# A compositional interaction network on one core: all four full steps of its first layer in high and low halves, and a summation tree whose first level is done by accumulating transfers

## The chip, the core and the metric

The kernel runs on one core of a Trainium2 chip. The metric is device time in microseconds (us) of one execution: 946.62 us, the median of three runs (946.28 to 947.04). The profile is of one further execution, which took 947.22 us, of which the recorded span is 945.3 us.

## The reference

For 512 samples, 32 embeddings of 32 numbers are gathered from 32 tables. Two layers of a compositional interaction network follow, and a three-layer perceptron:

```python
e = jnp.stack([tbl_0[ids[:, 0]], ..., tbl_31[ids[:, 31]]], axis=1)      # (512, 32, 32)
x0 = prev = e
for W in (filter_0, filter_1):                # (1, 32*32, 128), (1, 32*128, 128)
    z = jnp.einsum('bhd,bmd->bhmd', x0, prev).reshape(b, h * m, d)
    cur = jax.nn.relu(jnp.einsum('bpd,pn->bnd', z, W[0]))
    prev = cur; outs.append(cur)
z = jnp.sum(jnp.concatenate(outs, axis=1), axis=-1)                      # (512, 256)
h = jnp.concatenate([z, dense_ctx], axis=1)
h = jnp.maximum(h @ W_top1 + b_top1, 0.0)
h = jnp.maximum(h @ W_top2 + b_top2, 0.0)
y = h @ W_top3
```

All of it is float32. A product of two float32 matrices can be had on TensorE in one float32 instruction pair, or as three passes in the type fp32r, where each factor is split into a high part (the value rounded to fp32r) and a low part (the rest): high x high, low x high, high x low.

## The kernel before

The batch is cut into 4 blocks of 128 samples, the embedding dimension into 8 groups of 4; that makes 32 chunks of 4 x 128 = 512 columns. While chunk c is in layer 2, chunk c+1 is in layer 1 and chunk c+2 is being fetched and spread. Every engine runs an order that is written out by hand in slots.

**Layer 2.** A chunk has two halves q = 0 and 1 (a "pair" of tiles ab = 0, 1, each 128 samples wide), a half has four rounds e = 0 to 3, and a round has four slots for TensorE: slot 16q + 4e + 2ab + kind. In each TensorE multiplies cur (128 x 128) with 512 columns of the second filter in three passes (line 836) into a bank. Kind 0 banks go to ScalarE, which scales four 128-column pieces by a field of x0 and puts them side by side in parts (line 521); its slots are 16q + 4e + ab. Kind 1 banks go to VectorE, which adds its eight scaled pieces of a round into acc (line 721); its slots are 16q + 4e. The last of VectorE's additions of a half lands in parts too. ScalarE has one bank per tile, VectorE two, so TensorE may be about two rounds ahead of VectorE. Each half leaves two tiles of parts, 128 x 2048, whose 16 pieces of 128 must be summed: GpSimd halves each three times (line 352: 1024, 512 and 256 wide), which leaves two pieces, called left. parts has two buffers, so ScalarE may write the same buffer again two halves later, once the first level has read it (the wait on tree). In the next chunk ScalarE copies one piece of left into a bank (line 455, slot 20), VectorE adds the other (line 623, slot 24) and folds the rectified total into sum2 (line 629, slot 28).

**Layer 1.** Five steps. VectorE multiplies the fields by a shifted copy of them (line 587; step 1 in slot 0, steps 2 and 3 in slot 4, the half step 0 in slot 8, step 4 in slot 12). Steps 1 and 2 (SPLIT) are then split: ScalarE writes the high part (line 461, slots 5 and 13), GpSimd the low part (line 363), and TensorE takes three fp32r passes. Steps 3 and 4 are multiplied in float32 (line 774). Step 0 is written into cur_bank itself, ScalarE takes its high part (line 466, slot 9) and VectorE its low part in place (low16, line 591, slot 12), and one fp32r pass does. All five products accumulate in cur_bank (slots 17, 19, 21, 23 and 24), so the first of them may not start before low16 has read the bank (pe_product waits on low16 at the first step of its order). After the last, ScalarE writes cur_high (line 472, slot 25) and VectorE cur_low (line 598, slot 28) for the chunk's own layer 2, whose slots 0 and 1 wait for them. VectorE's slot 0 then sums the bank (line 606).

GpSimd also gathers the next block's rows (line 378, four gathers a chunk) and SyncE sends the turned fields to DRAM and loads them back in shifted copies (x4 and five of shifts, 256 KB each).

At the end the last tile's tree is done by VectorE (line 738), the one before it by GpSimd; VectorE needs both for the last total (line 743), and TensorE turns its result for the perceptron.

Of the kernel before, what the change touches and what calls it, by code (L numbers as in the profile page):

```python
# [27 lines left out]
P = 128  # L28
# [12 lines left out]
TREE = 3  # L41
LEFTS = 2
# [5 lines left out]
SPLIT = (1, 2)  # L48
# [5 lines left out]
ACT_PAIR_HIGH = {5: 1, 13: 2}  # L54
ACT_HIGH16, DVE_LOW16 = 9, 12
PE_PRODUCT = {17: 1, 19: 3, 21: 0, 23: 4, 24: 2}
# [7 lines left out]
ACT_TURN, PE_TURN, ACT_TURNED = 1, 6, 8  # L64

ACT_LEFT, DVE_TOTAL, DVE_FOLD = 20, 24, 28
# [7 lines left out]
def dlrm_tower(nc, ids, tables, w0_ab, w0_ba, w0_half, w1, w_top1, b_top1, w_top2, b_top2, w_top3, dense_t,  # L74
               identity, parity, x0_dram, out):
    ctx = ExitStack()
    with ctx:
# [39 lines left out]
        half = sb("half", [P, 1024 + 512])  # L117
# [8 lines left out]
        z1 = sb("z1", [P, B])  # L126
# [5 lines left out]
        lefts = free[:, 0:LEFTS * DC * 2 * N2].rearrange("p (i t l n) -> p i t l n", i=LEFTS, t=DC, l=2)  # L132
        left = [lefts[:, i, :, :, :] for i in range(LEFTS)]
# [194 lines left out]
        def _(pool):  # L328
# [611 lines left out]
```

## Time and profile before

| | |
|---|---|
| median of three runs | 946.62 us |
| the profiled execution | 947.22 us, span 945.3 us |
| TensorE busy | 881.0 us (93%), granted clock 0.998 |
| VectorE busy | 765.0 us (81%) |
| ScalarE busy | 691.3 us (73%) |
| GpSimd busy | 773.2 us (82%) |
| transfers | 58.13 MB, 18.6% of the 16 DMA engines by SyncE's queue, 1.4% by GpSimd's |

Busy times are the union of an engine's instructions, and in the timelines below an instruction's own duration reaches into the next one's, so that costs are read as the distance from start to start. The share of an engine says little here, since the four are coupled slot by slot; what has to be followed is the order of starts within one chunk.

### The profile page before, as it was taken

What the parts mean: (1) busy time and instruction counts of PE and PEld (TensorE: products, weight loads), DVE (VectorE), ACT (ScalarE), POOL (GpSimd) and SP (SyncE); (2) the same over time, 40 slices, a digit from 0 to 9 for tenths busy, and PEclk for the clock granted to TensorE, in tenths of its full rate; (3) what the DMA queues carried; (4) which work ended last, traced back from release to release, by engine and by line L of the source; (5) the groups of instructions that cost most, each with busy time, mean ns of one, the idle gap of its engine ahead of it and who ended that gap; (6) DMA issues with size and microseconds to landing.
All of it is one profiled execution on the core that took longest, in us unless ns stands there. A gap on an engine that the chain in (4) does not pass through costs nothing.

```text
span 945.3 us, 17955 instructions
## 1 busy us (share of the span) xinstructions
PE 881.0 (93%) x3551; PEld 650.2 (69%) x3551; DVE 765.0 (81%) x2391; ACT 691.3 (73%) x2347; POOL 773.2 (82%) x582
## 2 busy tenths in 40 slices
PE   0289999999999999999999999999999999999989
PEld 0157777777777777777777777777777777777753
DVE  4068888889888888898888889988888899888893
ACT  2058777787878777878787778787877777877762
POOL 7768899888888999988889989887777877777772
PEclk9999999999999999999999999999999999999999
DMA  6031222222112222221122222211222222102000
GB/s 175 13 105 51 75 75 75 73 72 71 32 50 70 73 74 73 74 71 34 46 69 74 73 74 74 74 38 37 67 71 71 71 71 71 47 29 66 1 1 0
DMA packets 41436, 58.13 MB, mean 61 GB/s; under 512 B 7265, under 2 KB 16033, under 8 KB 41410
## 3 DMA queue, kind: packets, MB, share of 16 engines
q1 hardware_dynamic: 37314, 55.76, 18.6%
q0 software_dynamic: 4096, 2.11, 1.4%
q14 instruction: 20, 0.16, 0.1%
q8 instruction: 6, 0.10, 0.0%
HBM read 54.79 MB, written 3.05 MB: 61 GB/s over the span
## 4 chain that ended last, share of the span: by engine, by line
PE 53%; DVE 26%; issue 14%; POOL 4%; DVEq 2%; DMA 0%; ACT 0%
PE bank L836 38%; DVE acc L721 18%; PE bank L774 12%; POOL rows L331 4%; DVE pair L587 4%; DVE cur_low L598 2%; DVE parts L721 1%; DVEq L718 1%; PE bank L879 1%; DVEq L240 0%; PE bank L866 0%; PE bank L867 0%; DVE sum L629 0%; PE bank L874 0%; DVEq L707 0%
## 5 line engine op out<-in xcount | busy, mean ns | idle before, releaser
L521 ACT ACTIVATE parts<-bank,x 128x128 f32<-128x128 f32 x2048 | 584.8, 385 | 143.5 <-PE bank L836 140.1
L721 DVE SCALAR_TENSOR_TENSOR acc<-bank,x,acc 128x128 f32<-128x128 f32 x1792 | 485.6, 343 | 97.2 <-PE bank L836 96.0
L836 PE MATMUL bank<-w_high,cur_high 128*128 128x512 f32 x1024 | 440.5, 430 | 10.9 <-DVE acc L721 10.0
L836 PE MATMUL bank<-w_low,cur_high 128*128 128x512 f32 x1024 | 401.4, 392 | 0.0
L836 PE MATMUL bank<-w_high,cur_low 128*128 128x512 f32 x992 | 389.1, 392 | 0.0
L352 POOL TENSOR_TENSOR half<-parts 128x1024 f32<-128x1024 f32 x127 | 307.1, 2418 | 92.4 <-DVE parts L721 91.9
L836 PEld LDWEIGHTS bank<-w_high,cur_high 128*128 128x128 f32 x1024 | 192.5, 188 | 105.9 <-DVE acc L721 29.3
L836 PEld LDWEIGHTS bank<-w_low,cur_high 128*128 128x128 f32 x1024 | 193.0, 188 | 48.8 <-issue 14.8
L836 PEld LDWEIGHTS bank<-w_high,cur_low 128*128 128x128 f32 x992 | 186.4, 188 | 41.8
L352 POOL TENSOR_TENSOR half<-half 128x512 f32<-128x512 f32 x127 | 165.5, 1303 | 10.0
L378 POOL DMA_INDIRECT rows_next<-table_dram,ids_next x96 | 92.5, 963 | 17.5 <-issue 7.0
L352 POOL TENSOR_TENSOR w_sb<-half 128x256 f32<-128x256 f32 x127 | 94.0, 740 | 11.2 <-POOL half L352 2.5
L363 POOL TENSOR_TENSOR pair_low<-pair,pair_high 128x512 fp32r<-128x512 f32 x62 | 80.2, 1294 | 9.1 <-ACT pair_high L461 5.9
L587 DVE TENSOR_TENSOR pair<-bank,shifts 128x512 f32<-128x512 f32 x124 | 82.0, 682 | 4.4 <-DMA shifts<-x_scratch 4.4
L774 PE MATMUL bank<-pair,w_sb 128*128 128x512 f32 x132 | 66.9, 592 | 0.0
L721 DVE SCALAR_TENSOR_TENSOR acc<-bank,x,parts 128x128 f32<-128x128 f32 x128 | 41.6, 347 | 17.3 <-PE bank L836 15.7
L788 PE MATMUL bank<-w_high 128*128 128x512 f32 x26 | 8.6, 491 | 40.8 <-DMA rows<-table_dram,ids_sb 40.8
L331 POOL DMA_INDIRECT rows<-table_dram,ids_sb x32 | 34.2, 1069 | 12.1 <-issue 9.4
L466 ACT CAST pair_hl<-bank 128x512 fp32r<-128x512 f32 x32 | 18.8, 588 | 31.7 <-DVE bank L587 31.6
L461 ACT CAST pair_high<-pair 128x512 fp32r<-128x512 f32 x62 | 40.7, 657 | 0.1
L721 DVE SCALAR_TENSOR_TENSOR parts<-bank,x,acc 128x128 f32<-128x128 f32 x128 | 38.5, 342 | 0.0
L788 PEld LDWEIGHTS bank<-w_high 128*128 128x128 f32 x26 | 6.1, 247 | 42.9 <-issue 41.6
(77 smaller groups left out, 485.8 us busy)
## 6 DMA issues: line engine op xcount, KB each, us to landing
shifts<-x_scratch SPq DMA_DIRECT2D x155, 256.0 KB
x<-x_scratch SPq DMA_DIRECT2D x31, 256.0 KB, 2.9
x_scratch<-turned SPq DMA_DIRECT2D x31, 64.0 KB, 1.5
rows_next<-table_dram,ids_next POOLq DMA_INDIRECT x96
wt<-w_top_dram SPq DMA_DIRECT2D x2, 512.0 KB, 8.9
x_scratch<-turned SPq DMA_DIRECT2D x31, 32.0 KB, 1.8
rows<-table_dram,ids_sb POOLq DMA_INDIRECT x32, 2.4
w_sb<-w_ab_dram SPq DMA_DIRECT2D x1, 256.0 KB
```

What stands on the lines that cost most here:

```text
L331: nc.gpsimd.indirect_dma_start(out=rows[:, 0, f, :], out_offset=None, in_=tables[f], in_offset=bass.IndirectOffsetOnAxis(ids_sb[:, 0, f:f ...
L352: nc.gpsimd.tensor_tensor(dst, src[:, 0:width], src[:, width:2 * width], ALU.add).then_inc(tree, 1)
L363: nc.gpsimd.tensor_tensor(pair_low[step][:], pair[step - 1][:], pair_high[step][:].bitcast(FP32), ALU.subtract).then_inc(pair_low_done, 1)
L378: nc.gpsimd.indirect_dma_start(out=rows_next[:, f, :], out_offset=None, in_=tables[f], in_offset=bass.IndirectOffsetOnAxis(ids_next[:, f:f ...
L461: nc.scalar.copy(pair_high[step][:], pair[step - 1][:]).then_inc(pair_high_done, 1)
L466: nc.scalar.copy(pair16_hl[:], pair16_bank(c)[:]).then_inc(high16, 1)
L521: ins = nc.scalar.activation(parts[q][ab][:, at:at + N2], act_bank[ab][:, i * N2:(i + 1) * N2], ACT.Copy, scale=x0[u][:, h, 2 * q + ab:2 * ...
L587: nc.vector.tensor_tensor(dst[:], fields, shifted, ALU.mult).then_inc(paired, 1)
L598: nc.vector.scalar_tensor_tensor(out=cur_low[u][:], in0=cur_bank[:], scalar=0.0, in1=cur_high[u][:].bitcast(FP32), op0=ALU.max, op1=ALU.su ...
L721: nc.vector.scalar_tensor_tensor(out=dst, in0=dve_bank[e % 2 * 2 + ab][:, i * N2:(i + 1) * N2], scalar=x0[u][:, h, 2 * q + ab:2 * q + ab + ...
L774: ins = nc.tensor.matmul(cur_bank[:], filters, products, start=step == order[0] and i == 0, stop=step == order[-1] and i == len(terms) - 1)
L836: return nc.tensor.matmul(dst[:], cur_half[u][:, cols], w1_half[:, fields], **flags)
```

## The change

SPLIT takes in all four full steps. ScalarE writes four high parts (slots 4, 8, 9 and 16) and the first is one slot earlier, GpSimd writes four low parts, and TensorE does steps 3 and 4 in three fp32r passes too. ScalarE's high part of step 0 moves from slot 9 to 12, VectorE's low16 from slot 12 to 16, and the products from slots 17, 19, 21, 23, 24 (steps 1, 3, 0, 4, 2) to 18, 19, 21, 22, 24 (steps 1, 2, 3, 0, 4). The turn of the next fields is in slots 0, 4 and 5 in place of 1, 6 and 8.

The tree's first level is taken from GpSimd's arithmetic: a new function add_halves waits for a whole half, and starts two transfers within the on-chip memory that add the upper 1024 columns of a tile's parts to the lower (512 KB each). GpSimd then does two levels (512 and 256 wide) once the transfer has landed, and a new addition, sum_left, that gives a chunk's total. ScalarE copies that into the bank with the rectifier (slot 20), and VectorE has only the fold left, in slot 24 in place of 28.

```diff
-SPLIT = (1, 2)
+SPLIT = (1, 2, 3, 4)
...
-ACT_PAIR_HIGH = {5: 1, 13: 2}
-ACT_HIGH16, DVE_LOW16 = 9, 12
-PE_PRODUCT = {17: 1, 19: 3, 21: 0, 23: 4, 24: 2}
+ACT_PAIR_HIGH = {4: 1, 8: 2, 9: 3, 16: 4}
+ACT_HIGH16, DVE_LOW16 = 12, 16
+PE_PRODUCT = {18: 1, 19: 2, 21: 3, 22: 0, 24: 4}
...
-ACT_TURN, PE_TURN, ACT_TURNED = 1, 6, 8
-
-ACT_LEFT, DVE_TOTAL, DVE_FOLD = 20, 24, 28
+ACT_TURN, PE_TURN, ACT_TURNED = 0, 4, 5
+
+ACT_TOTAL, DVE_FOLD = 20, 24
...
+            def add_halves(pair_no, q, whole):
+
+                pool.wait_ge(act_prod, (pair_no + 1) * (2 * EACH))
+                pool.wait_ge(mac, (pair_no + 1) * (2 * MACS))
+                nc.gpsimd.tensor_tensor(mark[:], mark[:], mark[:], ALU.subtract)
+                width = EACH * HG * N2 // 2
+                for ab in range(2 if whole else 1):
+                    nc.gpsimd.dma_start(parts[q][ab][:, 0:width], parts[q][ab][:, width:2 * width],
+                                        accum_op=ALU.add).then_inc(added[ab], 16)
+
             def sum_parts(chunk, pair_no, t):
 
                 tile = pair_no * 2 + t % 2
-                src, width, at = parts[t // 2 % 2][t % 2], EACH * HG * N2 // 2, 0
-                if t % 2 == 0:
-                    pool.wait_ge(act_prod, (pair_no + 1) * (2 * EACH))
-                    pool.wait_ge(mac, (pair_no + 1) * (2 * MACS))
-                for level in range(TREE):
-                    if level > 0:
-                        pool.wait_ge(tree, tile * TREE + level)
-                    if level == TREE - 1:
-                        dst = left[t // DC % LEFTS][:, t % DC, :, :].rearrange("p l n -> p (l n)")
-                        if t % DC == 0:
-                            pool.wait_ge(left_free, chunk + 1)
-                    else:
-                        dst = half[:, at:at + width]
-                    nc.gpsimd.tensor_tensor(dst, src[:, 0:width], src[:, width:2 * width],
-                                            ALU.add).then_inc(tree, 1)
-                    src, at, width = dst, at + width, width // 2
+                pool.wait_ge(added[t % 2], (pair_no + 1) * 16)
+                src = parts[t // 2 % 2][t % 2]
+                nc.gpsimd.tensor_tensor(half[t % 2][:], src[:, 0:512], src[:, 512:1024], ALU.add).then_inc(tree, 1)
+                pool.wait_ge(tree, tile * TREE + 1)
+                nc.gpsimd.tensor_tensor(left[:, t % DC, :, :].rearrange("p l n -> p (l n)"),
+                                        half[t % 2][:, 0:256], half[t % 2][:, 256:512], ALU.add).then_inc(tree, 1)
+
+            def sum_left(chunk):
+
+                pool.wait_ge(tree, (chunk + 1) * (DC * TREE))
+                pool.wait_ge(total_rectified, chunk + 1)
+                nc.gpsimd.tensor_tensor(total.rearrange("p (t n) -> p t n", t=DC), left[:, :, 0, :], left[:, :, 1, :],
+                                        ALU.add).then_inc(totalled, 1)
 
             def pair_lows(c, which):
 
...
+                for t in range(0, tiles, 2):
+                    whole = next_block or t < tiles - 2
                     if t % DC == 0 and (next_block or t < tiles - DC):
+                        pair_lows(k * CPB + t // DC + 1, (2, 3))
+                    add_halves(k * (tiles // 2) + t // 2, t // 2 % 2, whole)
+                    for s in (t, t + 1):
+                        if (next_block and s < rows_at) or (one_after and s > rows_at):
+                            for f in late[s]:
+                                gather(f)
+                    if t % DC == 2 and (next_block or t < tiles - DC - 2):
+                        pair_lows(k * CPB + t // DC + 2, (0, 1))
+                    for s in (t, t + 1) if whole else (t,):
+                        sum_parts(k * CPB + t // DC, k * (tiles // 2) + t // 2, s)
+                        if s % DC == DC - 1:
+                            sum_left(k * CPB + t // DC)
+                        if next_block and s == rows_at:
...
-        def act_left(act, c, u, pairs_before):
-
-            act.wait_ge(tree, (c + 1) * (DC * TREE))
+        def act_total(act, c, pairs_before):
+
+            act.wait_ge(totalled, c + 1)
             act.wait_ge(paired, pairs_before)
-            nc.scalar.copy(x4_bank[:].rearrange("p (t n) -> p t n", t=DC),
-                           left[u][:, :, 0, :]).then_inc(left_copied, 1)
+            nc.scalar.activation(x4_bank[:], total, ACT.Relu).then_inc(total_rectified, 1)
 
...
-        def dve_total(dve, c, u):
-
-            dve.wait_ge(left_copied, c + 1)
-            half_total = x4_bank[:].rearrange("p (t n) -> p t n", t=DC)
-            nc.vector.tensor_tensor(half_total, half_total, left[u][:, :, 1, :], ALU.add).then_inc(left_free, 1)
-
-        def dve_fold(dve, c, k, total):
-
-            dve.wait_ge(left_free, c + LEFTS + 1)
-            s2 = sum2[:, bass.ds(k, 1), :, :].rearrange("p o t n -> p (o t n)")
-            nc.vector.scalar_tensor_tensor(
-                out=s2, in0=total, scalar=0.0, in1=s2, op0=ALU.max, op1=ALU.add).then_inc(folded, 1)
+        def block_sum(k):
+
+            return sum2[:, bass.ds(k, 1), :, :].rearrange("p o t n -> p (o t n)")
+
+        def dve_fold(dve, c, k):
+
+            dve.wait_ge(total_rectified, c + 2)
+            nc.vector.tensor_tensor(block_sum(k), x4_bank[:], block_sum(k), ALU.add).then_inc(folded, 1)
 
         @block.vector
...
```

VectorE, the first half of a chunk and the start of the second, before (acc in groups of eight are the rounds' additions, pair_hl is low16, bank<-bank,shifts is step 0):

```order
-L587 TENSOR_TENSOR pair<-bank,shifts 128x512 x2
-L721 SCALAR_TENSOR_TENSOR acc<-bank,x_0,acc 128x128 x8
-L587 TENSOR_TENSOR bank<-bank,shifts 128x512
-L721 SCALAR_TENSOR_TENSOR acc<-bank,x_0,acc 128x128 x8
-L587 TENSOR_TENSOR pair<-bank,shifts 128x512
-L591 TENSOR_TENSOR pair_hl<-bank,pair_hl 64x512
-L721 SCALAR_TENSOR_TENSOR acc<-bank,x_0,acc 128x128 x6
-L721 SCALAR_TENSOR_TENSOR parts<-bank,x_0,acc 128x128 x2
```

The same place now:

```order
+L597 TENSOR_TENSOR pair<-bank,shifts 128x512 x2
+L725 SCALAR_TENSOR_TENSOR acc<-bank,x_0,acc 128x128 x8
+L597 TENSOR_TENSOR bank<-bank,shifts 128x512
+L725 SCALAR_TENSOR_TENSOR acc<-bank,x_0,acc 128x128 x8
+L597 TENSOR_TENSOR pair<-bank,shifts 128x512
+L725 SCALAR_TENSOR_TENSOR acc<-bank,x_0,acc 128x128 x6
+L725 SCALAR_TENSOR_TENSOR parts<-bank,x_0,acc 128x128 x2
+L601 TENSOR_TENSOR pair_hl<-bank,pair_hl 64x512
```

low16 has gone behind the eight additions of the half's last round.

VectorE, the end of the second half, before (bank<-bank,w_sb is the total, the sum after cur_low is the fold; the names w_sb hold left and total, which lie in w1_sb, the buffer through which filter 1 was loaded):

```order
-L721 SCALAR_TENSOR_TENSOR acc<-bank,x_1,acc 128x128 x14
-L623 TENSOR_TENSOR bank<-bank,w_sb 128x512
-L721 SCALAR_TENSOR_TENSOR acc<-bank,x_1,acc 128x128 x8
-L598 SCALAR_TENSOR_TENSOR cur_low<-bank,cur_high 128x512
-L629 SCALAR_TENSOR_TENSOR sum<-bank,sum 128x512
-L721 SCALAR_TENSOR_TENSOR acc<-bank,x_1,acc 128x128 x6
```

And now:

```order
+L725 SCALAR_TENSOR_TENSOR acc<-bank,x_1,acc 128x128 x14
+L636 TENSOR_TENSOR sum<-bank,sum 128x512
+L725 SCALAR_TENSOR_TENSOR acc<-bank,x_1,acc 128x128 x8
+L608 SCALAR_TENSOR_TENSOR cur_low<-bank,cur_high 128x512
+L725 SCALAR_TENSOR_TENSOR acc<-bank,x_1,acc 128x128 x6
```

The total is gone and the fold stands in its place, so that only cur_low is left between the last two rounds.

GpSimd, one half of a chunk now (before, each tile had additions 1024, 512 and 256 wide, with one gather behind it):

```order
+L343 TENSOR_TENSOR mark<-mark 128x1
+L346 DMA parts<-parts 128x1024 x2
+L387 DMA rows_next<-table_dram,ids_next 128x32 x2
+L371 ISA
+L372 TENSOR_TENSOR pair_low<-pair,pair_high 128x512
+L371 REGISTER_ALU
+L372 TENSOR_TENSOR pair_low<-pair,pair_high 128x512
+L352 REGISTER_ALU
+L354 TENSOR_TENSOR half<-parts 128x512
+L355 ISA
+L356 TENSOR_TENSOR w_sb<-half 128x256
```

The two transfers are started first, then come the gathers and the low parts, and only then the additions that wait for them. In the other half the low parts stand ahead of the transfers, and nothing but the gathers is between these and the additions.

## Rows read from the trace of the kernel before

**Rows 1.** The page: busy time by engine, then the chain by engine.

```profile
PE 881.0 (93%) x3551; PEld 650.2 (69%) x3551; DVE 765.0 (81%) x2391; ACT 691.3 (73%) x2347; POOL 773.2 (82%) x582
...
PE 53%; DVE 26%; issue 14%; POOL 4%; DVEq 2%; DMA 0%; ACT 0%
```

**Rows 2.** The instructions of line 598: count, first and last start.

```profile
L598 DVE SCALAR_TENSOR_TENSOR cur_low<-bank,cur_high x32: 678/682/692, 56.4 to 892.1; 128x512 fp32r<-128x512 f32 x32
```

**Rows 3.** The timeline of VectorE: start us, us, instructions, [idle before].

```profile
513.38 2.16 DVE L721 SCALAR_TENSOR_TENSOR acc<-bank,x,acc 128x128 f32<-128x128 f32 x8 [1.53 <-PE bank L836]
...
516.06 0.68 DVE L629 SCALAR_TENSOR_TENSOR sum<-bank,sum 128x512 f32 x1
516.65 1.64 DVE L721 SCALAR_TENSOR_TENSOR acc<-bank,x,acc 128x128 f32<-128x128 f32 x6
...
525.85 2.15 DVE L721 SCALAR_TENSOR_TENSOR acc<-bank,x,acc 128x128 f32<-128x128 f32 x8
527.91 0.68 DVE L587 TENSOR_TENSOR pair<-bank,shifts 128x512 f32<-128x512 f32 x1
528.63 0.69 DVE L591 TENSOR_TENSOR pair_hl<-bank,pair_hl 64x512 fp32r<-64x512 f32 x1
...
540.18 2.16 DVE L721 SCALAR_TENSOR_TENSOR acc<-bank,x,acc 128x128 f32<-128x128 f32 x8 [1.53 <-PE bank L836]
```

**Rows 4.** The timeline of TensorE in the second half of a chunk.

```profile
529.58 0.47 PE L774 MATMUL bank<-pair_high,w_high 128*128 128x512 f32 x1 [0.19 <-DVE pair_hl L591]
...
530.35 0.39 PE L836 MATMUL bank<-w_high,cur_high 128*128 128x512 f32 x1
...
531.04 0.40 PE L836 MATMUL bank<-w_high,cur_high 128*128 128x512 f32 x1
...
531.74 1.02 PE L774 MATMUL bank<-pair,w_sb 128*128 128x512 f32 x2
...
532.82 0.39 PE L836 MATMUL bank<-w_low,cur_high 128*128 128x512 f32 x1
```

**Rows 5.** The timeline of ScalarE around its slots 9 to 16.

```profile
526.05 0.59 ACT L466 CAST pair_hl<-bank 128x512 fp32r<-128x512 f32 x1 [1.06 <-DVE bank L587]
526.53 2.18 ACT L521 ACTIVATE parts<-bank,x 128x128 f32<-128x128 f32 x8
528.54 0.68 ACT L461 CAST pair_high<-pair 128x512 fp32r<-128x512 f32 x1
529.05 1.22 ACT L521 ACTIVATE parts<-bank,x 128x128 f32<-128x128 f32 x4
```

**Rows 6.** GpSimd's groups by line: busy us, mean ns, idle before.

```profile
L352 POOL TENSOR_TENSOR half<-parts 128x1024 f32<-128x1024 f32 x127 | 307.1, 2418 | 92.4 <-DVE parts L721 91.9
L352 POOL TENSOR_TENSOR half<-half 128x512 f32<-128x512 f32 x127 | 165.5, 1303 | 10.0
L378 POOL DMA_INDIRECT rows_next<-table_dram,ids_next x96 | 92.5, 963 | 17.5 <-issue 7.0
L352 POOL TENSOR_TENSOR w_sb<-half 128x256 f32<-128x256 f32 x127 | 94.0, 740 | 11.2 <-POOL half L352 2.5
L363 POOL TENSOR_TENSOR pair_low<-pair,pair_high 128x512 fp32r<-128x512 f32 x62 | 80.2, 1294 | 9.1 <-ACT pair_high L461 5.9
```

**Rows 7.** Transfers: KB each, median us to landing; then a stretch of loads.

```profile
x<-x_scratch SPq DMA_DIRECT2D x31, 256.0 KB, 2.9
x_scratch<-turned SPq DMA_DIRECT2D x31, 64.0 KB, 1.5
...
wt<-w_top_dram SPq DMA_DIRECT2D x2, 512.0 KB, 8.9
```

```profile
500.50:503.50 3.00, 2.80 (x11) 1.72 (x10) 2.94 (x9) 2.97 (x11) 2.74 (x3) 1.00 0.92 274
```

**Rows 8.** The timeline of GpSimd, then of VectorE, after the last round.

```profile
921.45 3.39 POOL L352 TENSOR_TENSOR half<-parts 128x1024 f32<-128x1024 f32 x1 [3.10 <-DVE parts L721]
```

```profile
927.48 0.69 DVE L743 TENSOR_TENSOR parts<-w_sb 128x512 f32<-128x512 f32 x1 [0.69 <-POOL w_sb L352]
```

More of the change, by code:

```diff
@@ L116, in dlrm_tower @@
         parts = [[sb(f"parts_{i}{j}", [P, EACH * HG * N2]) for j in range(2)] for i in range(2)]
-        half = sb("half", [P, 1024 + 512])
+        half = [sb(f"half_{i}", [P, 512]) for i in range(2)]
+        mark = sb("mark", [P, 1])
         sum2 = sb("sum2", [P, BLOCKS, DC, N2])
@@ L131, in dlrm_tower @@
         z1_half = free[:, (H1 + H2) // P * B:][:, 0:BLOCKS * 2 * P].rearrange("p (k h b) -> p k h b", k=BLOCKS, h=2)
-        lefts = free[:, 0:LEFTS * DC * 2 * N2].rearrange("p (i t l n) -> p i t l n", i=LEFTS, t=DC, l=2)
-        left = [lefts[:, i, :, :, :] for i in range(LEFTS)]
+        left = free[:, 0:DC * 2 * N2].rearrange("p (t l n) -> p t l n", t=DC, l=2)
+        total = free[:, DC * 2 * N2:DC * 3 * N2]
         z2, y_sb = pair[1], pair[0][0:1, 0:B]
@@ L407, in _ @@
             pool.wait_ge(first_gathered[0], (F - LAST_TABLES) * 16)
             pool.wait_ge(first_gathered[1], LAST_TABLES * 16)
-            nc.gpsimd.memset(half[:, 0:1], 0.0).then_inc(rows_ready, 1)
+            nc.gpsimd.memset(mark[:], 0.0).then_inc(rows_ready, 1)
+            pool.wait_ge(rows_ready, 1)
             fetch_ids(1)
@@ L412, in _ @@
                 gather(f)
-            pair_lows(1, (0,))
+            pair_lows(1, (0, 1))
             with pool.Fori(0, BLOCKS - 2) as k:
@@ L534, in body @@
                                     act_turn(act, c + 2)
-                                if slot == ACT_LEFT and not (first and u == 0):
-                                    act_left(act, c - 1, 1 - u,
-                                             CHUNKS * STEPS if last and u == UNROLL - 1 else (c + 2) * STEPS)
+                                if slot == ACT_TOTAL and not (first and u == 0):
+                                    act_total(act, c - 1,
+                                              CHUNKS * STEPS if last and u == UNROLL - 1 else (c + 2) * STEPS)
                                 if slot == ACT_X4 and not last:
@@ L582, in dve_pair @@
                 wait(dve, multiplied, products_before(c, step))
-                if step in SPLIT:
-                    wait(dve, pair_low_done, (c - 2) * len(SPLIT) + SPLIT.index(step) + 1)
                 dst = pair[step - 1]
@@ L683, in body @@
                                 dve_sum(dve, c)
-                            if slot == DVE_TOTAL and not (first and u == 0):
-                                dve_total(dve, c - 1, 1 - u)
                             if not (last and u == UNROLL - 1):
@@ L729, in _ @@
             src, width = parts[CPAIRS - 1][1], EACH * HG * N2 // 2
-            for level in range(TREE):
+            for level in range(LAST_TREE):
                 if level == 0:
@@ L752, in pe_turn, with pe_product @@
             nc.tensor.transpose(turn_bank[:, 0:P], turn_in[:], ident[:]).then_inc(transposed, 1)
-        def pe_product(pe, c, step, order=PRODUCT_ORDER, turn=True):
+        def pe_product(pe, c, step, order=PRODUCT_ORDER):
             if step == order[0]:
-                wait(pe, summed, c)
-                if turn:
-                    pe.wait_ge(turned_ready, c + 1)
-                if pair16_bank(c) is cur_bank:
-                    pe.wait_ge(low16, c + 1)
+                pe.wait_ge(low16, c + 1)
             if step == 0:
-                pe.wait_ge(low16, c + 1)
                 terms = [(w0_half_hl[:], pair16_hl[:])]
@@ L847, in body @@
                                 if slot in PE_PRODUCT and not (last and u == UNROLL - 1):
-                                    pe_product(pe, c + 1, PE_PRODUCT[slot], turn=not last)
+                                    pe_product(pe, c + 1, PE_PRODUCT[slot])
                                 if slot == PE_TURN and not last:
```

69 lines of the change are left out of this document (31 added, 38 removed).

## The prediction

> **What bounds the kernel now.** I read the page first: TensorE is busy for 93% of the span, but the chain that ended last runs through it for only 53% and through VectorE for 26%, with 14% of issue [rows 1]. So neither is the bound alone: they hand the chain to each other once per chunk, and the reader is to see where. The instructions of line 598, one per chunk, start from 56.4 to 892.1 us, so a chunk takes 835.7 / 31 = 26.96 us on average [rows 2]. Then the timelines of one chunk, engine by engine.
>
> VectorE starts its round e = 2 of the second half (slot 24) at 513.38 after 1.53 us of idle, released by TensorE, and again at 540.18: 26.80 us later [rows 3]. From there it has no idle time until its slot 16: cur_low, fold, a round, sum, step 1, a round, steps 2 and 3, a round, step 0, a round, step 4, and low16, which starts at 528.63 [rows 3]. TensorE idles for low16 and starts the first product at 529.58 [rows 4]. From that product on TensorE has no stall; its slot 27 releases VectorE at 540.18 [rows 3]. The loop is thus closed, and its three pieces are 528.63 - 513.38 = 15.25 (VectorE), 529.58 - 528.63 = 0.95 (low16 and its hand-over), and 540.18 - 529.58 = 10.60 (TensorE from product to slot 27): 26.80. Whatever lies on these pieces counts in full; the rest has slack. GpSimd was idle for 91.9 us waiting for the ends of the halves [rows 6], so it had some 1.4 us a half to spare.
>
> **The change, part by part.**
>
> *Products of steps 3 and 4.* A float32 product costs 532.59 - 531.74 = 0.85 us (the pass at 532.82 is the second of its slot, 0.23 behind the first), a slot of three passes 531.04 - 530.35 = 0.69 [rows 4]. Both are on TensorE's piece: 2 x 0.16 = -0.32.
>
> *Product 1 from slot 17 to 18.* Slot 18 now comes ahead of the product, in TensorE's wait, and not between it and slot 27: -0.69 [rows 4]. TensorE's piece becomes 10.60 - 0.32 - 0.69 = 9.59.
>
> *Total gone, fold from slot 28 to 24.* The total was done in the idle time ahead of slot 24 and the fold now stands there; what leaves the chain is the fold between the rounds of slots 24 and 28, 516.65 - 516.06 = -0.59 [rows 3]. The fold waits for ScalarE's slot 20, as the total did in the same place.
>
> *low16 from slot 12 to 16.* This is the part that speaks against the change. cur_bank holds step 0 until low16 has read it, so the first product waits for low16 wherever that stands. It now starts behind the round of eight additions of slot 12, 527.91 - 525.85 = +2.06 [rows 3]. Step 4 is followed by a round instead of by low16, which waited 0.12 more than the usual 0.60: I take -0.07. VectorE's piece becomes 15.25 - 0.59 + 2.06 - 0.07 = 16.65.
>
> Loop now: 16.65 + 0.95 + 9.59 = 27.19, which is +0.39 us a chunk. TensorE, done with slot 18 at about 15.8, stands idle for nearly 2 us there. 30 chunks have such a loop: +11.7 us.
>
> *ScalarE.* Two more high parts, 529.05 - 528.54 = 0.51 each [rows 5]. Its slot 9 was done at 526.05 - 1.06 = 524.99 and it then idled for step 0 [rows 5]. Now two high parts (1.02), slot 12's four pieces (2.01 / 2 = 1.00, half of the way from high16's end at 526.53 to 528.54) and high16 itself (0.48) follow: high16 ends near 527.5, and low16 would start at 513.38 + 16.65 = 530.0. So 2.5 us are to spare; if that cover were gone, each further microsecond would count.
>
> *GpSimd.* Gone: four additions of 2.42. Added: two low parts of 1.29, one addition 512 wide for the total, 1.30, and four starts of a transfer, which the trace shows for gathers only, at 0.96 [rows 6]; a start can't be below zero, and I take 0.96. The round of a chunk is 4 x (1.30 + 0.74) + 4 x 1.29 + 1.30 + 4 x 0.96 (gathers) + 4 x 0.96 = 22.3, and with the gaps of before, (10.0 + 11.2 + 17.5 + 9.1) / 32 = 1.5, 23.8 us [rows 6]. To that comes each landing that nothing covers. In the first half only two gathers and the second start stand between the first transfer and its addition, 2.9 us; in the second half the low parts do too, 5.5 us. No row shows an accumulating transfer within the memory. From below, a load of half the size lands in 2.9 us; from above, the 512 KB weight loads in the crowded start landed in 8.9 [rows 7]. 64 KB in 1.5 and 256 KB in 2.9 give 0.0073 us per KB and so 4.8 for 512 KB. I take 4.8, being nearest to these. Then 1.9 us are uncovered, the second tile's transfer (another 512 KB at 274 GB/s, 1.9 us [rows 7]) lands under the first tile's additions, and the round is 25.7 + 0.3 for a wait on ScalarE = 26.0. That is below 27.19, so GpSimd is not the bound. Behind its wait for a transfer are queued, in the second half, the total, the low parts of steps 3 and 4 and the next starts; TensorE needs low part 3 some 21 us into the loop, and it is written by 19.1. With 2.9 the round is 24.1; with 8.9 it would be past 33.
>
> The Trainium skill, DMA: Bandwidth & Descriptors, section on the anatomy of one DMA on the GpSimd path, fits a time of 2.0 us plus the bytes at 436 GB/s, an estimate of 3.2 us for 512 KB. By that figure the end would cost 1.6 us less than by mine; no run so far shows which.
>
> *The end.* GpSimd started the last tile it does at 921.45 and VectorE took it up at 927.48, 6.0 us later [rows 8]. Now it is 0.2 (the mark) + 0.96 + 4.8 + 1.30 + 0.74 and gaps = 8.1: +2.1 (from +0.2 with 2.9, to +6.2 with 8.9). TensorE waits for it, so it counts.
>
> Sum against the profiled execution: 947.22 + 11.7 + 2.1 = 961.0; the median was 0.6 below that execution, so 960.4. I say 960.
>
> **Rivals.**
>
> *A, GpSimd becomes the bound (slower still).* Its round passes 27.19 when a lone transfer lands later than about 5.8 us. For: an accumulation reads the destination as well, so twice the reading. Against: the transfers are alone on the 16 engines for most of the time. At 6.2 us, 3.3 + 0.7 us are uncovered and the round is 23.8 + 0.3 + 4.0 = 28.1, with the second transfer of a half late too about 28.4: +1.6 in the 24 chunks with gathers, +0.4 in six, +3.5 at the end: 947 + 38 + 2 + 4 = 991. The Trainium skill, same page, rules for kernel authors, says that an accumulate reads its destination and writes it later; it gives no rate, and nothing here shows one.
>
> *B, faster.* VectorE's rounds are slowed today by GpSimd's long additions from the same memory, and with the 1024-wide ones gone they shorten. For: GpSimd's own addition of that kind took 3.39 in place of 2.42 when VectorE added from the same memory at the end [rows 6, 8], so the two can hold each other up. Against: the rounds take 2.06 to 2.08 wherever I look, and they read a bank. VectorE's piece now has six rounds, so this decides from 0.39 / 6 = 0.065 us a round. At 0.16 us a round the loop is 27.19 - 0.96 = 26.23: 947 - 17 + 2 = 932.
>
> *C, no change.* low16's late place costs less than a whole round, for instance because step 4 and low16 hide each other's start; the loop is 26.8 and the end +0 to +2: 946 to 949.
>
> **Chances.** Forecast 0.55, with its own range of 953 to 968 (0.15 us a chunk either way, and the bounds of the end); A 0.22; B 0.13; C 0.10. The range for 8 in 10 leaves out most of B, below 938 (0.09), and half of A, above 990 (0.11). A change below 0.2% (1.9 us) can't be told from none in a measurement of this kernel. Faster: B and 0.02 of C, 0.15. Same: 0.07 of C. Slower: the rest, 0.78.
>
> **What would show it.** Right: on VectorE low16 starts 16.6 us after the round of slot 24, TensorE is idle for about 2 us ahead of its first product, released by low16, and the instructions of cur_low are 27.3 us apart. Products of three passes take 0.70. GpSimd waits for a transfer once a chunk, under 3 us. A: GpSimd busy or waiting on transfers through the whole chunk, and TensorE or ScalarE released by GpSimd. B: rounds below 2.0 us. I am wrong if TensorE doesn't wait for low16, or if a chunk is shorter than 26.8 us.

## The result, and the profile after

The changed kernel takes 963.18 us (median of four runs, 962.77 to 964.87) beside 946.45 for the kernel before on the same chip: a ratio of 1.018, 95% interval 1.0163 to 1.0198. Forecast were 960 us and slower. The profiled execution was the longest of the four, 964.87 us; its span went from 945.3 to 963.0 us, +17.7. One execution of before_low16_late took 2248.89 us beside three of 988.9 to 990.9 and is left out below.

The page of the changed kernel, busy time and chain by engine, and two rows of its groups (busy us, mean ns of one | idle before, and whom it waited for):

```profile
PE 857.5 (89%) x3613; PEld 668.5 (69%) x3613; DVE 736.7 (77%) x2360; ACT 714.6 (74%) x2409; POOL 714.3 (74%) x739
...
PE 49%; DVE 28%; issue 14%; POOL 5%; DVEq 2%; ACT 1%; DMA 1%; POOLq 0%; ACTq 0%
...
L354 POOL TENSOR_TENSOR half<-parts 128x512 f32<-128x512 f32 x127 | 164.4, 1295 | 64.8 <-DMA parts<-parts 64.6
...
L775 PE MATMUL bank<-pair_high,w_high 128*128 128x512 f32 x124 | 52.1, 420 | 54.3 <-DVE pair_hl L601 53.3
```

TensorE's products, VectorE and GpSimd are busy for less time than in [rows 1], and yet the kernel is longer: the time is in a wait. TensorE idles 53.3 us for pair_hl, which is low16. In [rows 4] the same place had 0.19 of idle time.

VectorE over one chunk (start us, us, instructions, [idle before]); it answers to [rows 3]:

```profile
513.77 0.69 DVE L601 TENSOR_TENSOR pair_hl<-bank,pair_hl 64x512 fp32r<-64x512 f32 x1
516.39 0.61 DVE L725 SCALAR_TENSOR_TENSOR acc<-bank,x,parts 128x128 f32<-128x128 f32 x2 [1.93 <-PE bank L837]
...
520.78 2.16 DVE L725 SCALAR_TENSOR_TENSOR acc<-bank,x,acc 128x128 f32<-128x128 f32 x8 [2.22 <-PE bank L837]
522.86 0.68 DVE L636 TENSOR_TENSOR sum<-bank,sum 128x512 f32 x1
524.25 2.16 DVE L725 SCALAR_TENSOR_TENSOR acc<-bank,x,acc 128x128 f32<-128x128 f32 x8 [0.72 <-PE bank L837]
526.33 0.68 DVE L608 SCALAR_TENSOR_TENSOR cur_low<-bank,cur_high 128x512 fp32r<-128x512 f32 x1
...
541.03 0.69 DVE L601 TENSOR_TENSOR pair_hl<-bank,pair_hl 64x512 fp32r<-64x512 f32 x1
```

and TensorE where it waits:

```profile
541.86 0.49 PE L775 MATMUL bank<-pair_high,w_high 128*128 128x512 f32 x1 [1.75 <-DVE pair_hl L601]
```

From low16 to low16 are 541.03 - 513.77 = 27.26 us, against the forecast 27.19. The pieces are 541.03 - 524.25 = 16.78 on VectorE (forecast 16.65), 541.86 - 541.03 = 0.83 to the product (0.95), and 524.25 - 514.60 = 9.65 on TensorE (9.59; its product of that chunk started at 514.60).

The instructions of cur_low, which answer to [rows 2], are now 848.9 / 31 = 27.38 us apart, +0.42 a chunk:

```profile
L608 DVE SCALAR_TENSOR_TENSOR cur_low<-bank,cur_high x32: 677/683/691, 60.5 to 909.4; 128x512 fp32r<-128x512 f32 x32
```

So the 17.7 us are 4.1 ahead of the first cur_low (60.5 for 56.4), 13.2 in the 31 intervals, and 0.4 behind the last. The 4.1 I had not forecast.

The mean of 0.42 hides that the intervals are not alike. One by one, from cur_low to cur_low, they are in turns 26.80 and 27.08 us before and 27.25 and 27.54 now, so 28 of the 31 grew by 0.44 to 0.52, by 0.46 on average. The first shrank from 28.93 to 26.65, the second grew by 0.90, and the ninth took 28.79 for 27.07, +1.72. In the ninth GpSimd's program goes from the first block to the second:

```profile
297.59 2.51 POOL L372 TENSOR_TENSOR pair_low<-pair,pair_high 128x512 fp32r<-128x512 f32 x2 [3.58 <-issue]
```

GpSimd stood still for 3.58 us ahead of the low parts of steps 3 and 4 without a wait that the profile shows, and TensorE waited 1.0 us for one of them. Counted from the second cur_low (87.2 for 85.3), the 17.7 us are 1.9 up to there, 15.4 in 30 intervals and 0.4 at the end.

**The start.** pe_product now waits for low16 ahead of any chunk's first product; before, it did so only where the product's bank is the one that low16 reads, which in chunk 0 it isn't. Of before, then of after:

```profile
51.88 3.60 PE L774 MATMUL bank<-pair,w_sb 128*128 128x512 f32 x8
```

```profile
54.21 5.40 PE L775 MATMUL bank<-pair,w_sb 128*128 128x512 f32 x8 [2.22 <-DVE pair_hl L601]
```

The wait is 2.2 us, and the products behind it take 5.40 in place of 3.60; the granted clock was 0.83 in the stretch from 50 to 60 us, 1.00 before the change. But the kernel before had a stretch of low clock too, a little later: it was 0.50 from 66 to 68 us, after TensorE had waited 1.91 us for VectorE at 64.89. And the first interval, 28.93 us long before and 26.65 now, makes good 2.3 of the 4.1 us: 1.9 are left at the second cur_low. Experiments 9 and 10 take the two apart.

**The end.** Three things nearly cancel. GpSimd after its last wait for VectorE, and VectorE's total behind it, which answer to [rows 8]:

```profile
935.56 1.24 POOL L343 TENSOR_TENSOR mark<-mark 128x1 f32<-128x1 f32 x1 [0.57 <-DVE parts L725]
936.74 0.88 POOL L346 DMA_DIRECT2D parts<-parts  x1
941.35 1.26 POOL L354 TENSOR_TENSOR half<-parts 128x512 f32<-128x512 f32 x1 [3.73 <-DMA parts<-parts]
```

```profile
943.52 0.69 DVE L746 TENSOR_TENSOR parts<-w_sb 128x512 f32<-128x512 f32 x1 [5.59 <-POOL w_sb L356]
```

943.52 - 935.56 = 7.96, forecast 8.1, before 6.03: +1.9. TensorE idles 1.88 us ahead of its last transpose, and from 944 to 953 us its clock was 0.79 to 0.83 (1.00 in the same place before), so what follows the total takes 963.0 - 943.5 = 19.5 where it took 945.3 - 927.5 = 17.8: +1.7. And the last chunk got shorter by 3.2 (909.4 to 935.56 is 26.2, 892.1 to 921.45 was 29.4), mostly because two of VectorE's additions with both inputs in the on-chip memory no longer meet GpSimd's 1024-wide ones: 3.2 us together. The total and a fold that are gone from this stretch (1.2) and new idle time of VectorE (0.9) nearly cancel. The two additions, before and then after:

```profile
900.23 3.37 DVE L696 TENSOR_TENSOR w_sb<-sum 128x1024 f32<-128x1024 f32 x1
...
909.24 2.61 DVE L616 TENSOR_TENSOR rows_next<-w_sb 128x384 f32<-128x384 f32 x1
```

```profile
917.53 2.26 DVE L700 TENSOR_TENSOR w_sb<-sum 128x1024 f32<-128x1024 f32 x1
...
925.44 0.56 DVE L626 TENSOR_TENSOR rows_next<-w_sb 128x384 f32<-128x384 f32 x1
```

GpSimd's additions that they met ended at 902.51 and 911.43 before; the first of the two now meets a 512-wide one that ended at 918.71, the second none. So VectorE was done 1.1 us after GpSimd with the wide one, both times, and 0.4 us after it with the narrow one.

### The profile page after: what moved, and what is told of

Read it like the earlier page. It is cut to its first block, busy times and chain, and to the rows that moved or that the text cites. A ratio compares the mean times of both kernels' runs of the same rounds, so it can differ in the third digit from the quotient of the medians.

```text
span 963.0 us, 18096 instructions
## 1 busy us (share of the span) xinstructions
PE 857.5 (89%) x3613; PEld 668.5 (69%) x3613; DVE 736.7 (77%) x2360; ACT 714.6 (74%) x2409; POOL 714.3 (74%) x739
## 3 DMA queue, kind: packets, MB, share of 16 engines
q0 software_dynamic: 22384, 68.70, 38.1%
q1 hardware_dynamic: 37314, 55.76, 18.2%
## 4 chain that ended last, share of the span: by engine, by line
PE 49%; DVE 28%; issue 14%; POOL 5%; DVEq 2%; ACT 1%; DMA 1%; POOLq 0%; ACTq 0%
PE bank L837 36%; DVE acc L725 18%; PE bank L775 11%; POOL rows L334 3%; DVE pair L597 3%; DVE parts L725 2%; DVE pair_hl L601 2%; DVEq L722 1%; PE bank L880 1%; ACT parts L534 1%; DVE cur_low L608 1%; PE bank L875 0%; DMA parts<-parts 0%; PE bank L843 0%; POOL half L354 0%
## 5 line engine op out<-in xcount | busy, mean ns | idle before, releaser
L837 PE MATMUL bank<-w_high,cur_high 128*128 128x512 f32 x1024 | 407.1, 398 | 1.2 <-ACT cur_high L485 0.7
L354 POOL TENSOR_TENSOR half<-parts 128x512 f32<-128x512 f32 x127 | 164.4, 1295 | 64.8 <-DMA parts<-parts 64.6
L372 POOL TENSOR_TENSOR pair_low<-pair,pair_high 128x512 fp32r<-128x512 f32 x124 | 158.4, 1297 | 29.4 <-ACT pair_high L474 25.4
L346 POOL DMA_DIRECT2D parts<-parts x127 | 115.4, 1069 | 4.5 <-issue 4.5
L775 PE MATMUL bank<-pair_high,w_high 128*128 128x512 f32 x124 | 52.1, 420 | 54.3 <-DVE pair_hl L601 53.3
L474 ACT CAST pair_high<-pair 128x512 fp32r<-128x512 f32 x124 | 80.1, 646 | 0.0
L775 PEld LDWEIGHTS bank<-pair_high,w_high 128*128 128x128 f32 x124 | 23.2, 187 | 71.6 <-issue 60.3
L343 POOL TENSOR_TENSOR mark<-mark 128x1 f32<-128x1 f32 x64 | 14.2, 222 | 73.4 <-DVE parts L725 73.4
L775 PE MATMUL bank<-pair_high,w_low 128*128 128x512 f32 x124 | 48.9, 395 | 0.0
L775 PE MATMUL bank<-pair_low,w_high 128*128 128x512 f32 x124 | 48.9, 394 | 0.0
```

Source lines behind the costliest of these rows:

```text
L346: nc.gpsimd.dma_start(parts[q][ab][:, 0:width], parts[q][ab][:, width:2 * width], accum_op=ALU.add).then_inc(added[ab], 16)
L354: nc.gpsimd.tensor_tensor(half[t % 2][:], src[:, 0:512], src[:, 512:1024], ALU.add).then_inc(tree, 1)
L372: nc.gpsimd.tensor_tensor(pair_low[step - 1][:], pair[step - 1], pair_high[step][:].bitcast(FP32), ALU.subtract).then_inc(pair_low_done, 1)
L474: nc.scalar.copy(pair_high[step][:], pair[step - 1]).then_inc(pair_high_done, 1)
L775: ins = nc.tensor.matmul(cur_bank[:], filters, products, start=step == order[0] and i == 0, stop=step == order[-1] and i == len(terms) - 1)
L837: return nc.tensor.matmul(dst[:], cur_half[u][:, cols], w1_half[:, fields], **flags)
```

## The experiments

Theory 1 is the prediction's: the first product waits for low16, and that closes the loop of a chunk. Theory 2, the rival: the time went to GpSimd, which now waits 64.6 us for transfers. Times are medians; the kernel before is at 946.5 to 947.2 in all comparisons. "Chunk" is the mean distance of the cur_low instructions in the profile. In most of a run the intervals have two lengths in turns, some 0.3 us apart (experiment 8 is the exception), and "a typical interval" is the shorter of the two.

**1. low16_early: low16 back ahead of the round.**

```diff
-ACT_HIGH16, DVE_LOW16 = 12, 16
+ACT_HIGH16, DVE_LOW16 = 12, 12
```

> The changed kernel with VectorE's low16 back in slot 12, ahead of the round of additions; everything else stays. Theory 1 (the first product waits for low16, and that wait closes the loop of a chunk): VectorE's piece loses a round, 2.06 us, TensorE's idle time ahead of its first product (1.7 us a chunk) is gone, and the chunk is then set by TensorE's own 25.3 us or by GpSimd's round, which without its 2.3 us of idle is about 25.0 to 26; about 25.6 us a chunk, 911 us in all (905 to 930). Theory 2 (the time went to the transfers and to GpSimd, which now waits 64.6 us for them): low16's place hardly matters, 955 to 965 us.

Measured: 909.04 us, ratio to before 0.9593 (0.9566 to 0.962); chunk 25.65. One number turns +1.8% into -4.1%. The chunk is the 25.6 that theory 1 gave; theory 2 is out as the cause. Its VectorE:

```profile
509.19 0.68 DVE L597 TENSOR_TENSOR pair<-bank,shifts 128x512 f32<-128x512 f32 x1
509.90 0.69 DVE L601 TENSOR_TENSOR pair_hl<-bank,pair_hl 64x512 fp32r<-64x512 f32 x1
510.63 1.65 DVE L725 SCALAR_TENSOR_TENSOR acc<-bank,x,acc 128x128 f32<-128x128 f32 x6
```

TensorE starts its product at 510.93 without idle time. What sets the chunk now is to be seen in the chain of the page, by engine:

```profile
PE 71%; POOL 16%; issue 7%; DVE 4%; DMA 1%; POOLq 0%; ACT 0%; DVEq 0%
```

VectorE has all but left it, and GpSimd, which had 5% of the changed kernel's chain, most of it in the gathers of the start, is in it. Not in every chunk, though: a typical interval is 25.25 us, and the mean of 25.65 comes from a few, above all the ninth with 30.28 us, in which TensorE waited for a low part and then ran at a clock of 0.50 from 285 to 287 us (in the nineteenth, of 27.20 us, it waited 1.4 us for one):

```profile
283.39 0.50 PE L775 MATMUL bank<-pair_high,w_high 128*128 128x512 f32 x1 [2.92 <-POOL pair_low L372]
```

**2. before_low16_late: the late place, with the first product in slot 18, in the kernel before.**

```diff
-ACT_HIGH16, DVE_LOW16 = 9, 12
-PE_PRODUCT = {17: 1, 19: 3, 21: 0, 23: 4, 24: 2}
+ACT_HIGH16, DVE_LOW16 = 9, 16
+PE_PRODUCT = {18: 1, 19: 3, 21: 0, 23: 4, 24: 2}
```

> The kernel before, with low16 moved from slot 12 to 16 and the first product from slot 17 to 18, and nothing else of the change. Theory 1: the loop gains a round and loses a slot of TensorE and 0.1 of step 4's wait, 2.06 - 0.69 - 0.1 = +1.3 us a chunk, 946.5 + 30 x 1.3 = 985 us (978 to 990). Theory 2: no change beyond 3 us, since neither transfers nor new work on GpSimd are there.

Measured: 989.40 us, 1.0447 (1.0423 to 1.0471); chunk 28.26, +1.30 as expected (a typical interval grew by 1.38). Of the 42.2 us that the span grew, 40.5 are in the intervals, 1.6 at the start (58.0 for 56.4) and 0.1 at the end. TensorE waits there too:

```profile
PE bank L774 <- DVE pair_hl L591: 47.3, 30, 1.7
```

**3. float_products: steps 3 and 4 in float32 again.**

```diff
-SPLIT = (1, 2, 3, 4)
-ACT_PAIR_HIGH = {4: 1, 8: 2, 9: 3, 16: 4}
+SPLIT = (1, 2)
+ACT_PAIR_HIGH = {4: 1, 8: 2}
...
-                    if t % DC == 0 and (next_block or t < tiles - DC):
-                        pair_lows(k * CPB + t // DC + 1, (2, 3))
```

> The changed kernel with only steps 1 and 2 in high and low parts, as before; steps 3 and 4 are float32 products again in the new slots, GpSimd and ScalarE lose two parts a chunk each; the tree by transfers stays. Theory 1: both products are in TensorE's piece, +0.32 us a chunk, 963 + 10 = 973 us (970 to 976). Theory 2: GpSimd's round loses 2.6 us a chunk and the kernel gets faster, below 955 us.

Measured: 970.69 us, 1.0241 (1.0224 to 1.0258); chunk 27.61, +0.23 for the expected +0.32; a typical interval grew by 0.26, and the ninth shrank from 28.79 to 27.80, without the low parts that came late there. GpSimd has 2.6 us less to do and the kernel is slower: it was not GpSimd.

**4. fold_late: the fold back in slot 28.**

```diff
-ACT_TOTAL, DVE_FOLD = 20, 24
+ACT_TOTAL, DVE_FOLD = 20, 28
```

> The changed kernel with VectorE's fold back in slot 28, between the last two rounds. Theory 1: it is in VectorE's piece again, +0.59 us a chunk, 963 + 18 = 981 us (977 to 984). Theory 2: VectorE has time to spare (77% busy), within 3 us of 963.

Measured: 978.44 us, 1.0319 (1.0296 to 1.0342); chunk 27.88, +0.50 for the expected +0.59; +0.54 in a typical interval.

**5. before_fold_early: only the fold moved, in the kernel before.**

```diff
-ACT_LEFT, DVE_TOTAL, DVE_FOLD = 20, 24, 28
+ACT_LEFT, DVE_TOTAL, DVE_FOLD = 20, 24, 24
```

> The kernel before, with nothing but the fold moved from slot 28 to 24, behind the total. Theory 1: the fold leaves VectorE's piece for the idle 1.53 us ahead of the round of slot 24: -0.59 us a chunk, 946.6 - 18 = 929 us (926 to 934), unless GpSimd's round, which had 1.4 us a half to spare, or ScalarE takes part of it. Theory 2 (only the loop's low16 mattered): 945 to 948.

Measured: 931.03 us, 0.9832 (0.9816 to 0.9849); chunk (876.3 - 56.1) / 31 = 26.46, -0.50. The same half microsecond from the other side: 16 us for one number, with none of the rest of the change.

**6. early_float_products: low16 early and float32 products.** The diffs of 1 and 3 together.

> The changed kernel with low16 in slot 12 and steps 3 and 4 as float32 products. TensorE has +0.32 us of its own a chunk, GpSimd 2.6 and ScalarE 1.0 less. If GpSimd's round sets the 25.65 us of that kernel, TensorE takes over at 25.25 + 0.32 = 25.6: 905 to 912 us, so the split of steps 3 and 4 is worth nothing. If TensorE sets it: +10, 919 us.

Measured: 912.43 us, 0.964 (0.9624 to 0.9656); chunk 25.69 against 25.65. The 95% intervals of this ratio and of low16_early's don't overlap, but only just. So once low16 is early, splitting steps 3 and 4 is worth 4.4 us by the ratios and 1.9 us by the two profiled executions, in place of the 10 that TensorE gains. The intervals say where the rest goes: a typical one is 0.33 us longer with float32 products, but the ninth is 4.4 shorter and the nineteenth 1.3. What TensorE gains by the split in nearly every chunk, late low parts take back in a few.

**7. no_transfer: low16 early, no transfers.** The upper 1024 columns of each tile are left out of the sum.

```diff
-                for ab in range(2 if whole else 1):
-                    nc.gpsimd.dma_start(parts[q][ab][:, 0:width], parts[q][ab][:, width:2 * width],
-                                        accum_op=ALU.add).then_inc(added[ab], 16)
...
-                pool.wait_ge(added[t % 2], (pair_no + 1) * 16)
```

> The changed kernel with low16 in slot 12, without the transfers and without the waits for them (the upper 1024 columns of each tile are left out of the sum). If GpSimd's round with its landings is what now sets the chunk of 25.65 us, TensorE's own 25.25 takes its place, and the end loses 4.6: 909 - 12 - 5 = 892 us (887 to 898). If TensorE already sets it and the transfers only sit at the end: 904.

Measured: 899.65 us, 0.9497 (0.9471 to 0.9522); chunk 25.42, and 50.3 us from the last cur_low to the end for 53.7. GpSimd's idle time, from its waits, is now at the ends of the halves, so it has left the path:

```profile
POOL mark L343 <- DVE parts L721: 148.5, 33, 6.9
```

The chain says the same:

```profile
PE 90%; POOL 5%; issue 2%; DVE 2%; DMA 0%; ACT 0%; POOLq 0%; ACTq 0%; DVEq 0%
```

The starts and landings thus cost 7.2 us in the intervals and 3.4 at the end, 10.6 between the two profiled executions and 9.4 between the medians, and not 17. TensorE's own 25.25 us was right for a typical interval, in both kernels: the median difference of two intervals is 0.01 us. Of the 7.2 us, 3.0 are in the ninth interval (30.28 against 27.27) and 1.7 in the nineteenth. So GpSimd does not set the chunk with low16 early; it comes late in some of them. My mistake was to read a mean of 25.65 as the length of each.

**8. arithmetic_tree: low16 early, first level by additions.**

```diff
+                nc.gpsimd.tensor_tensor(src[:, 0:1024], src[:, 0:1024], src[:, 1024:2048], ALU.add).then_inc(first_level, 1)
+                pool.wait_ge(first_level, tile + 1)
...
-                    nc.gpsimd.dma_start(parts[q][ab][:, 0:width], parts[q][ab][:, width:2 * width],
-                                        accum_op=ALU.add).then_inc(added[ab], 16)
```

> The changed kernel with low16 in slot 12 and the first level of the tree as GpSimd additions 1024 wide, in place, instead of transfers. If the transfers are what makes room for four low parts: GpSimd's round of 25.65 us loses four starts (3.9) and its waits for transfers (about 1) and gets four additions of 2.42 and their waits; about 30.5 us a chunk, 909 + 30 x 4.8 = 1050 us (1025 to 1065). If the transfers are dispensable: 905 to 915.

Measured: 1096.26 us, 1.156 (1.1525 to 1.1596); chunk 31.62 for the expected 30.5, and the time is above the range. The transfers, or something else that takes this work from GpSimd, are needed for the four low parts. Two things that I had not counted can be seen, and nothing here tells how much each adds: GpSimd's lateness comes back to it through the others, and TensorE's granted clock was 0.93 over the run, beside 0.99 and more in all other kernels:

```profile
PE bank L774 <- POOL pair_low L371: 128.1, 30, 5.9
ACT parts L533 <- POOL half L353: 120.6, 62, 2.9
...
POOL pair_low L371 <- ACT pair_high L473: 75.0, 47, 2.5
```

**9. start_guard: no wait for low16 in chunk 0's first product.**

```diff
             if step == order[0]:
-                pe.wait_ge(low16, c + 1)
+                if pair16_bank(c) is cur_bank:
+                    pe.wait_ge(low16, c + 1)
+                else:
+                    pe.wait_ge(turned_ready, 1)
```

> The changed kernel, with chunk 0's first product waiting for low16 only where it uses the bank that low16 reads, as before the change (in chunk 0 it doesn't); all other chunks unchanged. Theory 1: the 4.1 us that the first cur_low comes later (60.5 in place of 56.4) are this wait of 2.2 us and the lower clock that TensorE got behind it; 963 - 4 = 959 us, and the first cur_low is at 56.4. Theory 2 (the start is late because two more filters are split): no change, 963.

Measured: 961.96 us, 1.0159 (1.013 to 1.0187). The interval overlaps the changed kernel's, so the time alone doesn't tell. In the profile the wait is gone and the eight products take their 3.60 us again, but the transposes ahead of them took 1.97 for 1.09, at a clock of 0.50 from 50 to 52 us, and the first cur_low is at 58.4, not 56.4.

```profile
49.49 1.97 PE L810 MATMUL bank<-ident,parts 128*128 128x128 f32 x8 [2.09 <-DVE parts L675]
...
53.86 3.60 PE L779 MATMUL bank<-pair,w_sb 128*128 128x512 f32 x8
```

A trace with the wait and a clock of 1.00 from 50 to 60 us is that of experiment 10, whose edit is at the other end of the kernel:

```profile
54.24 3.70 PE L775 MATMUL bank<-pair,w_sb 128*128 128x512 f32 x8 [2.22 <-DVE pair_hl L601]
```

The first cur_low was at 56.4 without the wait and without low clock ahead of it (before), at 58.4 with the low clock only, at 58.8 with the wait only, at 60.5 with both. So the wait costs 2.1 to 2.4 us there and the low clock 1.7 to 2.0, and the low clock is not bound to the wait. Little of the wait stays, since the interval behind it is shorter where the wait was (26.7 us in place of 28.3 in this experiment): the second cur_low was at 86.7 here and at 87.2 in the changed kernel, 0.5 later, and at 85.5 with the wait only. These are single executions, but they say why taking the wait out gave no 4 us.

**10. end_busy: more products that keep TensorE busy ahead of its last transpose.**

```diff
-            keep_busy(6, dve_bank[1])
+            keep_busy(14, dve_bank[1])
```

> The changed kernel with 14 in place of 6 products that keep TensorE busy while it waits for the last total. Theory 1: the 1.9 us that TensorE is idle there lower its granted clock (0.79 to 0.83 behind it, 1.00 before the change), and that costs some 1.6 us beside the wait; 961.5 us. Theory 2: the time behind the wait has another cause; 963.

Measured: 961.56 us, 1.0154 (1.0131 to 1.0177), and the two intervals overlap again. In its profile the low clock is gone: from VectorE's total (941.34) to the end (959.2) are 17.9 us, 17.8 before the change, and the clock is 1.00 there throughout (the columns are the stretch, its length, busy us of PE, PEld, DVE, ACT and POOL, the clock, the share of DMA, GB/s):

```profile
944.00:948.00 4.00, 4.00 (x12) 2.07 (x11) 0.00 (x0) 2.15 (x4) 0.00 (x0) 1.00 0.01 2
```

The same stretch of the changed kernel:

```profile
944.00:948.00 4.00, 2.21 (x6) 1.56 (x7) 1.63 (x4) 0.27 (x1) 0.00 (x0) 0.79 0.00 0
```

That doesn't show that the added products keep the clock up. The trace of experiment 9 has 6 of them, and the same idle time as the changed kernel:

```profile
944.82 0.33 PE L787 MATMUL bank<-ident,rows_next 128*128 128x128 f32 x1 [1.87 <-DVE rows_next L626]
945.92 3.60 PE L879 MATMUL bank<-pair,wt 128*128 128x512 f32 x8
```

Its clock stayed at 1.00, and 17.8 us followed the total. Of the five traces with 1.86 to 1.89 us of idle time there, three had low clock behind it (the changed kernel, experiments 1 and 6) and two had not (4 and 9); of the three traces with 14 products (10, 11, 12) none had. That agrees with theory 1 and is too little to show it.

**11. all_three: low16 early, with the edits of 9 and 10.** The diffs of 1, 9 and 10 together.

> The changed kernel with low16 in slot 12, the wait of chunk 0 only where its bank is used, and 14 products that keep TensorE busy at the end. If the three are independent: 909 - 4.1 - 1.6 = 903 us (901 to 906).

Measured: 907.56 us, 0.9583 (0.9558 to 0.9609), above the range. It is only 1.5 us below low16_early, where 5.7 were expected, and the intervals of the two ratios overlap; the gain of the small edits isn't shown by it. Experiments 9 and 10 say why: neither small edit gives 4.1 or 1.6 us in each execution.

**12. half_first: that kernel, with step 0's product ahead of step 3's.**

```diff
-PE_PRODUCT = {18: 1, 19: 2, 21: 3, 22: 0, 24: 4}
+PE_PRODUCT = {18: 1, 19: 2, 21: 0, 23: 3, 24: 4}
```

> The same, with step 0's product in slot 21 and step 3's in slot 23, so that the third low part may come later. With low16 early, TensorE waited 9.4 us for low parts; if that is on the path, up to 9 us less than the kernel without this edit, 894 to 901 us; if GpSimd's round sets the chunk by itself, within 2 us of it.

Measured beside all_three: 901.67 us against 907.56, ratio to before 0.9538 (0.9509 to 0.9567); chunk 25.50 against 25.64. The intervals of the two ratios overlap a little, and single executions reach from 900.6 to 907.5 here and from 906.4 to 909.9 there. Of the 5.7 us between the two profiled executions, 1.6 are ahead of the first cur_low, where all_three had a stretch of low clock and this one none; the rest is mainly in the ninth and the nineteenth interval, 1.6 each, where the low parts came late. It has the lowest median of the kernels here that compute everything, 45 us below the one before and 61 below the changed one.

## Why the prediction was right

*What bounds the kernel.* The loop VectorE, low16, TensorE was the right one: experiments 1 to 5 move each of its members, and the time follows by nearly the member's own size, in both kernels. The new slots of the turn and of the high parts were not moved by themselves.

*Products.* -0.32 a chunk forecast; taking it back gave +0.23, +0.26 in a typical interval. *Fold.* -0.59 forecast; +0.50 and -0.50 when moved alone, 0.54 and 0.52 in a typical interval. Both were a little too large.

*low16 and the first product.* +2.06, -0.69 and -0.07 forecast; in the kernel before, these alone gave +1.30 on the chunk, +1.38 in a typical interval. The step that carries the sign was right. Moved singly, the three parts add to +0.6, and together they gave +0.46; the 0.1 between is open.

*The sum of the loop.* +0.39 a chunk forecast, +0.42 measured. I counted 30 chunks; the 31 intervals of cur_low give 13.2 us for my 11.7. The mean is nearer than the typical +0.46 because the first interval shrank by 2.3 us, which has nothing to do with the loop.

*ScalarE.* As forecast, not on the path: high16 ended at 537.65, low16 started at 541.03.

*GpSimd.* Forecast was a round below 27.19, with one uncovered wait a chunk under 3 us, and 64.6 us of waits over 32 chunks are 2.0, in 55 waits, the longest 3.7. Experiments 1 and 7 show how near it was: with chunks of 25.25 us a few wait for its low parts. The landing that rival A needed didn't come. A transfer alone took 4.6 us from its start to the addition, where I had put 0.96 + 4.8.

The Trainium skill's fit for this path (DMA: Bandwidth & Descriptors, the section on the anatomy of one DMA on the GpSimd path) gave an estimate of 3.2 us; the trace has 4.61 from the beginning of the start and 3.73 from its end, both above it.

*The end.* +2.1 forecast for GpSimd's last tile, +1.9 measured, by two errors of one size: the transfer took 1.1 less, the mark (GpSimd's one-column addition ahead of a transfer), 0.2 in the loop, took 1.24 beside VectorE's additions. And two terms were missing, the low clock behind TensorE's idle time in this execution (+1.7), and the last chunk's shorter additions (-3.2). Rival B was thus real in one place: VectorE's additions with two inputs in the on-chip memory did speed up. Its rounds, which read a bank, didn't.

By the Trainium skill, SBUF — State Buffer, section SBUF: two separate sides, a GpSimd operation that reads that memory and a VectorE operation with two inputs from it exclude each other on a shared pair of ports. The trace agrees: VectorE's additions ended 0.4 and twice 1.1 us after the GpSimd addition that they met, the same addition took 2.61 and 0.56 us, and the rounds of 2.07 us stayed as they were.

*The start.* Missed altogether: a condition taken out of pe_product adds a wait in chunk 0, 2.1 to 2.4 us at the first cur_low and 0.5 at the second. The rest of the 4.1 us is low clock, which other executions of the same start don't have. Taken out by itself the wait gave 961.96 us, no clear difference.

*The total.* For the profiled execution 961.0 us were forecast and 964.87 measured, 3.9 more: 1.9 up to the second cur_low, 3.7 in the 30 intervals behind it (15.4 for 11.7), and -1.7 at the end (0.4 for 2.1). The median of the four executions, 963.18, is 1.7 below it and 2.8 above the 960.4 of my sum. That the sum is this near is in part luck, since the end was too large for reasons that I had not seen. The sign and most of the size come from the loop.

## What to carry to other kernels

Where engines run in fixed slots, find the closed loop of waits, write its period as a sum of pieces, and ask of each moved instruction whether it is on a piece and what now stands ahead of it; here an instruction of 0.7 us, moved behind one of 2.1, took back more than two float32 products and a fold had gained. A change that bundles many moves should be tried one number at a time: one of its numbers cost 54 us, and one was worth 16 by itself. And look at the intervals one by one before you divide a time by the number of chunks: a mean that is 0.2 us longer can be a few chunks that are 1 to 3 us longer. Read conditions that a diff drops, too: a wait that is free in the steady state may cost at the start.

## What the runs showed of the hardware

The accumulating transfers within the on-chip memory: 127 of 512 KB kept the 16 engines busy for 38.1% of 963 us, which is 68.7 MB (2 of them gathers) / 367 us = 187 GB/s; SyncE's loads and stores ran at 55.76 MB / 175 us = 318 GB/s. Per byte written an accumulation costs 1.7 times as much. One alone, started at 936.74, was there at 941.35; of two started together at 925.40 the first was there at 930.05 and the second at 932.92.

TensorE's clock fell after short idle times, but not after each. It was 0.50, the lower of its two levels of 1.2 and 2.4 GHz, from 56 to 58 us in the changed kernel, behind 2.22 us of idle time. Behind the same 2.22 us in experiment 10 it stayed at 1.00, and eight products took 3.70 us in place of 5.40. In the kernel before it was 0.50 from 66 to 68 us, behind 1.91 us of idle time, and stayed at 1.00 behind 2.35 us that ended at 49.02; in experiment 9 it was 0.50 from 50 to 52 us, behind 2.09 us that ended at 49.49. At the end, behind 1.86 to 1.89 us, it fell in three traces of five. A stretch of low clock cost 1.7 to 2.0 us at the start and 1.7 at the end. Where it falls differs from one execution to the next, so a difference of that size between two profiles has to be looked for in others before it is put down to an edit.
